# First expert layer of a graph network kernel: other PSUM banks, fewer unread products, result relus one group later

## The reference

```python
idx = argmax(norm(x) @ router_w.T + router_b)
h = relu(norm(x) @ W1[idx] + b1[idx])
x = x + relu(h @ W2[idx] + b2[idx])
```

## Time and profile before

| what | us |
|---|---|
| median of 3 runs (3088.12 to 3096.96) | 3088.62 |
| the profiled execution's own time | 3107.93 |
| its span | 3106.2 |
| from the first second product of the loop to the last, 19 steps from group to group (1905.00 to 2047.12) | 142.12 |

### The profile page before, as it was taken

One profiled execution on the slowest core, in us unless ns is written; L12 is line 12 of the kernel. 1 busy time (PEld: TensorE's weight loads), 2 busy tenths in 40 slices (PEclk: granted clock), 3 DMA queues, 4 the chain that ended last, 5 costly groups with the idle time before them and its releaser, 6 DMA issues. The chain is left out here.

```text
span 3106.2 us, 49414 instructions
## 1 busy us (share of the span) xinstructions
PE 2079.5 (67%) x13355; PEld 1574.6 (51%) x13356; DVE 1801.6 (58%) x4427; ACT 1371.4 (44%) x3064; POOL 1564.0 (50%) x1492
## 2 busy tenths in 40 slices
PE   8999116655565555655566546857133599999998
PEld 5555004443344433443444444645133388988887
DVE  5422226666565565665566884345488686656565
ACT  4555125554454544545454123523134664444443
POOL 0066645666666666666662313543650155555554
PEclk9999557777777877776777657978555599999999
DMA  7577434444444444444441632565442162222332
GB/s 232 206 269 280 158 90 110 131 122 116 126 123 120 130 119 123 127 119 120 122 121 37 168 107 82 140 140 133 98 114 65 35 183 49 45 47 46 49 48 27
DMA packets 194692, 363.31 MB, mean 117 GB/s; under 512 B 52783, under 2 KB 127126, under 8 KB 187983
## 3 DMA queue, kind: packets, MB, share of 16 engines
q0 software_dynamic: 78160, 187.31, 25.2%
q1 hardware_dynamic: 106126, 171.10, 16.5%
q10 hardware_dynamic: 10240, 2.95, 0.4%
HBM read 246.22 MB, written 117.28 MB: 117 GB/s over the span
## 5 line engine op out<-in xcount | busy, mean ns | idle before, releaser
L834 POOL DMA_INDIRECT sum_ring<-h_tab,gnn_edge_row x880 | 837.7, 952 | 484.9 <-issue 244.8
L1107 PE MATMUL sum_bank<-sum_ring,sum_one_hot 128*128 128x264 f32 x1760 | 619.0, 498 | 218.0 <-DVE nodes_acc L971 110.6
L1107 PEld LDWEIGHTS sum_bank<-sum_ring,sum_one_hot 128*128 128x128 f32 x1760 | 402.5, 244 | 348.9 <-issue 276.5
L878 ACT ACTIVATE sum_one_hot_T<-sum_distance,sum_pick_unit 128x1024 f16<-128x1024 bf16 x110 | 126.3, 1148 | 625.7 <-remote 616.8
L2243 POOL DMA_INDIRECT out_dram<-moe_y,slots_nodes x112 | 193.3, 1726 | 259.7 <-ACT moe_y L2265 237.7
L964 DVE TENSOR_TENSOR sum_ring<-sum_ring,sum_bank 128x1024 f32<-128x1024 f32 x220 | 266.5, 1212 | 94.1 <-ACT sum_ring L906 93.1
L885 ACT ACTIVATE sum_distance_by_lane<-all_iota,gnn_minus_local 128x128 bf16<-128x128 f32 x880 | 267.4, 386 | 0.1
L2417 PE MATMUL moe_bank<-moe_w_high,slots_early 128*128 x896 | 245.0, 273 | 6.8 <-DVE moe_w_low L1745 6.8
L2417 PE MATMUL moe_bank<-moe_w_high,moe_hidden_low 128*128 x896 | 245.1, 274 | 0.0
L2417 PE MATMUL moe_bank<-moe_w_low,slots_early 128*128 x896 | 245.1, 274 | 0.0
L2234 POOL DMA_INDIRECT moe_tile<-normal,slots_rows x116 | 136.4, 1176 | 188.5 <-PEq L71 134.5
(11 more groups left out here) (451 smaller groups left out, 4555.8 us busy)
## 6 DMA issues: line engine op xcount, KB each, us to landing
h_tab<-rows_h_rows SPq DMA_DIRECT2D x49, 1056.0 KB
sum_local_rows<-local_tab SPq DMA_DIRECT2D x110, 256.0 KB
slots_stage<-in_L_ffn_W_dram SPq DMA_DIRECT2D x14, 1024.0 KB
sum_ring<-h_tab,gnn_edge_row POOLq DMA_INDIRECT x880
mask_tab<-rows_masks POOLq DMA_DIRECT2D x7, 1560.0 KB
sum_masks<-mask_tab SPq DMA_DIRECT2D x28, 390.0 KB
results<-moe_tiles SPq DMA_DIRECT2D x80, 128.0 KB
g_tab<-gnn_rows_out SPq DMA_DIRECT2D x49, 132.0 KB
```

The costliest lines, as they stand in the source:

```text
L834: nc.gpsimd.indirect_dma_start(ring[:, t % (RING * ST), :], None, k.h_tab, bass.IndirectOffsetOnAxis(k.edge_row[:, t:t + 1], 0)).then_inc( ...
L1107: last = nc.tensor.matmul(sum_b[j][:, 0:W0], hot[:, m % 3, t, :], ring[:, m % RING * ST + t, :], start=(u == 0), stop=(u == G - 1))
```

## The change

The change touches `moe0` alone. The eight PSUM banks are given out anew: four to the transposes (bank u), two to the hidden values (bank 4 + u % 2), two to the second products (bank 6 + u % 2). So a tile's first products wait for the hidden relu of the tile two before (`h_ok.slot(n + u + 2)`), and its second product for the addition of the tile two before (`y_add.slot(n + u + 2)`); transposes no longer wait for additions, and second products no longer for the next group's splits. Of the unread products one is left ahead of the first products and two ahead of the second products, the latter now ahead of the wait for the hidden relu. `y` has eight slots, four of them in the space of the raw first weights. ACT's result relus are those of the group before, behind the columns of the next; the first two groups stand outside its loop, which then takes two groups in a turn, and the last four result relus stand behind the loop. DVE makes three splits, the first addition, the last split, and then the other three additions. SP's stores go round eight slots.

```diff
--- before.py
+++ after.py
@@ -1392,7 +1392,9 @@
         rows_ok = s.sem("slot_rows_ready")
         den = flat(route.work[:, :, :])[:, 0:NT * H0].rearrange("p (t h) -> p t h", h=H0)
         space = s.sb("tiles", [P, 12, D])
-        y, xi = (space[:, j * 4:(j + 1) * 4, :] for j in range(2))
+        xi = space[:, 4:8, :]
+        y_rows = [space[:, 0:4, :], flat(w1_in[:, :, :, :])[:, 0:4 * D].rearrange("p (u f) -> p u f", u=4)]
+        y = lambda u: y_rows[u // 4][:, u % 4, :]
         xT = [space[:, 8 + 2 * j:10 + 2 * j, :].rearrange("p u f -> p (u f)").bitcast(F16).rearrange("p (u f) -> p u f", u=4) for j in range(2)]
         spare = flat(route.pick[0][:, :, :])[:, 0:4 * D].rearrange("p (u f) -> p u f", u=4)
         taken = lambda u: (xi if u < 4 else spare)[:, u % 4, :]
@@ -1400,6 +1402,7 @@
         xn, xnT = space[:, 0:XN, :], space[:, XN:XN + 2, :]
         rw_n, rw = s.sb("router_natural", [E0, D]), s.sb("router", [P, DC, E0])
         rb = s.sb("router_bias", [P, E0])
+        x_bank, h_bank, y_bank = (lambda u: bank[u]), (lambda u: bank[4 + u % 2]), (lambda u: bank[6 + u % 2])
         w2 = s.sb("w2", [F0, E0, D])
         b1_n, b1, b2 = s.sb("b1_rows", [E0, F0]), s.sb("b1_T", [F0, E0]), s.sb("b2", [P, E0, D])
         x = b2[:, 0:AHEAD * CH, :].rearrange("p (n t) f -> p n t f", n=AHEAD)
@@ -1411,7 +1414,7 @@
         written = [s.sem(f"xn_written{u}") for u in range(XN)]
         route_ok, w1_hi, w1_ok = s.sem("route_ready"), s.sem("w1_high"), s.sem("w1_split")
         tile_in = [s.sem(f"tile_loaded{u}") for u in range(8)]
-        out_ok = Landed(s, "y_written", 4)
+        out_ok = Landed(s, "y_written", 8)
         x_ps = Count(s, "x_in_psum", 8)
         x_hi, x_ok, h_ps, h_ok, y_ps, y_add, y_ok = (Count(s, n, 4) for n in (
             "xT_high", "xT_split", "hidden_T_in_psum", "hidden_T_ready", "y_in_psum", "y_biased", "y_ready"))
@@ -1462,9 +1465,9 @@
             sp.dma_start(flat(b2[:, :, :]), v.broadcast_to([P, v.shape[1]])).then_inc(loaded_b, 16)
 
             def save(i, u):
-                y_ok.done(sp, i * 4 + u)
-                sp.dma_start(rows(k.ys0, (i * 4 + u) * P, P), y[:, u, :]).then_inc(out_ok.sems[u], 16)
-            turns(sp, T, 4, save)
+                y_ok.done(sp, i * 8 + u)
+                sp.dma_start(rows(k.ys0, (i * 8 + u) * P, P), y(u)).then_inc(out_ok.sems[u], 16)
+            turns(sp, T, 8, save)
             out_ok.all(sp, T)
 
         @block.scalar
@@ -1497,19 +1500,31 @@
 
             def columns(t, u):
                 x_ps.done(act, t)
-                nc.scalar.activation(xT[0][:, u, :], bank[2 * u + 1][:, D:2 * D], ACT.Copy, scale=XS).then_inc(x_hi.sem, 1)
+                nc.scalar.activation(xT[0][:, u, :], x_bank(u)[:, 0:D], ACT.Copy, scale=XS).then_inc(x_hi.sem, 1)
             for u in range(4):
                 columns(u, u)
-            with act.Fori(0, T // 4) as i:
-                e = registers(nc, mybir.EngineType.Activation, route.expert[0:1, bass.ds(i * 4, 4)], E0 - 1)
+            def rectify(t, u):
+                y_add.done(act, t)
+                nc.scalar.activation(y(u), y(u), ACT.Relu).then_inc(y_ok.sem, 1)
+
+            def group(n, half):
+
+                e = registers(nc, mybir.EngineType.Activation, route.expert[0:1, n:n + 4] if isinstance(n, int) else route.expert[0:1, bass.ds(n, 4)], E0 - 1)
                 for u in range(4):
-                    h_ps.done(act, i * 4 + u)
-                    nc.scalar.activation(hT[:, u, :], bank[2 * u][0:F0, 0:P], ACT.Relu, bias=col(b1, e[u]), scale=1.0 / (XS * WS)).then_inc(h_ok.sem, 1)
+                    h_ps.done(act, n + u)
+                    nc.scalar.activation(hT[:, u, :], h_bank(u)[0:F0, 0:P], ACT.Relu, bias=col(b1, e[u]), scale=1.0 / (XS * WS)).then_inc(h_ok.sem, 1)
                 for u in range(4):
-                    columns(i * 4 + 4 + u, u)
-                for u in range(4):
-                    y_add.done(act, i * 4 + u)
-                    nc.scalar.activation(y[:, u, :], y[:, u, :], ACT.Relu).then_inc(y_ok.sem, 1)
+                    columns(n + 4 + u, u)
+                if not isinstance(n, int) or n:
+                    for u in range(4):
+                        rectify(n - 4 + u, (4 * half + 4 + u) % 8)
+            for half in range(2):
+                group(half * 4, half)
+            with act.Fori(1, T // 8) as i:
+                for half in range(2):
+                    group(i * 8 + half * 4, half)
+            for u in range(4):
+                rectify(T - 4 + u, 4 + u)
 
         @block.vector
         def _(v):
@@ -1594,17 +1609,23 @@
 
             def column_rest(t, u):
                 x_hi.done(v, t)
-                nc.vector.scalar_tensor_tensor(xT[1][:, u, :], bank[2 * u + 1][:, D:2 * D], XS, xT[0][:, u, :], ALU.mult, ALU.subtract).then_inc(x_ok.sem, 1)
+                nc.vector.scalar_tensor_tensor(xT[1][:, u, :], x_bank(u)[:, 0:D], XS, xT[0][:, u, :], ALU.mult, ALU.subtract).then_inc(x_ok.sem, 1)
             for u in range(4):
                 column_rest(u, u)
-            with v.Fori(0, T // 4) as i:
-                e = registers(nc, mybir.EngineType.DVE, route.expert[0:1, bass.ds(i * 4, 4)], E0 - 1)
-                for u in range(4):
-                    column_rest(i * 4 + 4 + u, u)
-                for u in range(4):
-                    y_ps.done(v, i * 4 + u)
-                    out_ok.slot(v, i, u)
-                    nc.vector.tensor_tensor(y[:, u, :], bank[2 * u + 1][:, 0:D], col(b2, e[u]), ALU.add).then_inc(y_add.sem, 1)
+            def add(i, n, u, slot, expert):
+                y_ps.done(v, n + u)
+                out_ok.slot(v, i, slot)
+                nc.vector.tensor_tensor(y(slot), y_bank(u)[:, 0:D], col(b2, expert), ALU.add).then_inc(y_add.sem, 1)
+            with v.Fori(0, T // 8) as i:
+                for half in range(2):
+                    n = i * 8 + half * 4
+                    e = registers(nc, mybir.EngineType.DVE, route.expert[0:1, bass.ds(n, 4)], E0 - 1)
+                    for u in range(3):
+                        column_rest(n + 4 + u, u)
+                    add(i, n, 0, half * 4, e[0])
+                    column_rest(n + 7, 3)
+                    for u in range(1, 4):
+                        add(i, n, u, half * 4 + u, e[u])
 
         @block.tensor
         def _(pe):
@@ -1651,36 +1672,35 @@
                 u = slot % 4
                 pe.wait_ge(tile_in[slot], (i + 1) * 16)
                 for c in range(DC):
-                    last = nc.tensor.transpose(bank[2 * u + 1][:, D + c * P:D + (c + 1) * P], taken(slot)[:, c * P:(c + 1) * P], k.ident[:, :])
+                    last = nc.tensor.transpose(x_bank(u)[:, c * P:(c + 1) * P], taken(slot)[:, c * P:(c + 1) * P], k.ident[:, :])
                 last.then_inc(x_ps.sem, 1)
 
-            def unread(m):
+            def unread(to, m):
 
                 for _ in range(m):
-                    nc.tensor.matmul(bank[0][:, P:2 * P], k.ident[:, :], k.ident[:, :], start=True, stop=True)
+                    nc.tensor.matmul(to, k.ident[:, :], k.ident[:, :], start=True, stop=True)
 
             def four(n, i, half):
 
                 e = registers(nc, mybir.EngineType.PE, route.expert[0:1, bass.ds(n, 4)], E0 - 1)
                 for u in range(4):
-                    h_ok.slot(pe, n + u)
+                    h_ok.slot(pe, n + u + 2)
                     if u == 0:
-                        unread(2)
+                        unread(h_bank(u)[:, P:2 * P], 1)
                     x_ok.done(pe, n + u)
                     for part, (pw, px) in enumerate(passes):
                         for c in range(DC):
-                            last = nc.tensor.matmul(bank[2 * u][0:F0, 0:P], col(w1[pw][:, c], e[u]), xT[px][:, u, c * P:(c + 1) * P],
+                            last = nc.tensor.matmul(h_bank(u)[0:F0, 0:P], col(w1[pw][:, c], e[u]), xT[px][:, u, c * P:(c + 1) * P],
                                                     start=(part == 0 and c == 0), stop=(part == 2 and c == DC - 1))
                     last.then_inc(h_ps.sem, 1)
                 for u in range(4):
-                    y_add.slot(pe, n + u)
                     turn(i + half, 4 * (1 - half) + u)
                 for u in range(4):
+                    y_add.slot(pe, n + u + 2)
+                    if u == 0:
+                        unread(y_bank(u)[:, D:D + P], 2)
                     h_ok.done(pe, n + u)
-                    if u == 0:
-                        unread(4)
-                    x_ok.done(pe, n + 4 + u)
-                    nc.tensor.matmul(bank[2 * u + 1][:, 0:D], hT[:, u, :], col(w2, e[u]), start=True, stop=True).then_inc(y_ps.sem, 1)
+                    nc.tensor.matmul(y_bank(u)[:, 0:D], hT[:, u, :], col(w2, e[u]), start=True, stop=True).then_inc(y_ps.sem, 1)
             for u in range(4):
                 turn(0, u)
             with pe.Fori(0, T // 8) as i:
```

## The result

| | us |
|---|---|
| median after, 5 runs (3105.29 to 3119.86) | 3113.09 |
| median before, 5 runs (3086.71 to 3096.96) | 3088.62 |
| ratio | 1.008, 95% interval 1.0062 to 1.0098 |
| profiled execution after (span 3103.5) | 3105.29 |

The change costs 24.5 us. The profiled executions don't show that in their spans: the one of before took longer than any of its five timed runs (3107.93), the one of after is the shortest of its five. The rest of the program differs by more than the change between two executions, so the loop has to be compared with the loop. The 18 steps that took 132.26 before take 159.40 now, 27.1 more. The two groups ahead of them are 2.9 shorter in this execution and the tail behind them is 1.1 longer, so that the stage, from its first gather to the next stage's first load, takes 192.98 in place of 167.60, 25.4 more.

The account below looks back on a forecast made before the run. The tile loop, 7.35 us a group, was taken as set by a hold after each fourth gather. With release, relu, return and remaining products a group became 7.9; 0.55 more over 19 intervals gave +10.5, so 3099 us, range 3074 to 3118.

Parts of the forecast that it names:

- the hold: Work handed on by PE waits until about a microsecond after a group's fourth gather; now on first products, group 7.9 us.
- release at 6.54: The held hidden relu of tile 0 was to be let go 6.54 us after the group's transposes began.
- First transpose to second product 1.5: Start of a group: transposes and two unread products were to take 1.5 us in place of 2.60, so −1.1.
- Product 2 at 1.41: Second products: product 2, waiting for tile 0's addition, was to start 1.41 us into their phase.
- Without gathers about 7: The last stretch of the loop without gathers was to take about 7 us, not 6.25.
- the tail: End of the loop: the last four result relus were to follow the last additions as before, at no cost.
- the second products: With two banks, their phase was to take 2.6 us in place of 2.01, +0.6 a group.
- what follows the release: Relu and return 0.41 us, tile 3 0.36 after tile 2, next transposes 0.44 to 0.66 later.
- The lead that the sequencer loses: PE's sequencer at the expert numbers: 0 to +0.5 us a group, taken as +0.25, giving 7.05 without a hold.
- the clock: Rival: more PE pauses lower the granted clock below 1.00, 2.5 us more a group, +48, 3136 us; chance 0.09.
- Faster: Rival: the hold concerns additions alone and falls into slack, groups of 6.8, −10.5, 3078 us; chance 0.26.
- No difference: Rival: new relays cost what removed waits give, 7.3 a group, 3088 to 3093 us; chance 0.24.

Follow-up runs that it names:

- e2: Changed kernel with hidden values four deep again, turned tiles in pairs in two banks, second products still two deep: ratio 0.9993, steps of 7.36 us.
- e5: Changed kernel without its gathers of tiles, POOL only counting up: steps of 7.30 us, ratio 0.997, later layers working on other values.
- e3: Changed kernel with second products four deep again, turned tiles in pairs in two banks, hidden values still two deep: ratio 1.0068, steps of 8.48 us.
- e12: Changed kernel with four more unread products a group, put ahead of tile 2's first products where PE stops: ratio 1.007, steps of 8.61 us.
- e10: Changed kernel with hidden values and second products four deep, turned tiles and hidden values in pairs, six unread products: ratio 0.9941, steps of 6.66 us.
- e11: The four-deep arrangement with three unread products a group instead of six: ratio 0.9941, steps of 6.67 us.
- e9: Kernel before with only the result relus a group later and eight rows of y: ratio 0.9973, steps of 7.09 us.
- e14: Changed kernel with a group's gathers in two bursts of two: 3095.47 us against 3089.99 for before, one run each, steps of 7.83 us.
- e7: Changed kernel with hidden values four deep, second products two deep and six unread products: ratio 1.0005, steps of 7.63 us.

## Why the prediction was right, and too small

The sign, the place and the mechanism held; the size, 10.5, was less than half of the 24.5 measured, and one sign that the prediction gave for being wrong, a granted clock under 1.00, did show. The step as the prediction put it was: the hold falls on the first products, tile 2 can't start before the hidden relu of tile 0, release at 6.54, group 7.9. e2 (this relay undone) gives the whole loss back, e5 (the gathers taken away) gives it back in the steps of the loop, and e3 shows that PE merely waits longer there when it comes earlier.

*Terms that held.* First transpose to second product 1.5: 1946.59 − 1945.12 = 1.47. Product 2 at 1.41: 1947.99 − 1946.59 = 1.40. Release at 6.54: 6.59. Without gathers about 7: 7.05 (e5: 7.03 to 7.34 at a clock of 1.00).

*Put at nothing: the tail.* From the last group's second products to the next stage's first load it took 2054.08 − 2047.12 = 6.96 before and takes 2059.84 − 2051.78 = 8.06 now, 1.1 us more, once.

*Mis-sized without effect: the second products.* Their phase was put at 2.6 and takes 1949.69 − 1946.59 = 3.10. The first two tiles are still through PE before the release, so the group doesn't show it.

*Mis-sized: what follows the release.* Relu and return were put at 0.41; they take 1952.31 − 1951.71 = 0.60, since PE goes on 0.24 after the relu's end and not 0.05. From tile 2 to the next transposes I had 0.36 + 0.44 to 0.66, that is 0.80 to 1.02; at a clock of 1.00 it takes 1945.12 − 1944.00 = 1.12. The sum becomes 6.59 + 0.60 + 1.12 = 8.31, which e12 shows at 8.33 to 8.40. These 0.4 a group are some 8 us of the 19 steps. The lead that the sequencer loses was counted in the sum without a hold and left out of the sum with it.

*Mis-judged: the clock.* Its chance was 0.09 with 48 us; it fell in 13 of 18 steps, and cost little. The same 25 instructions take 2.59 at 1.00 and 3.71 at 0.58, but most of that is time that the release would have taken anyway: groups measured at their transposes take 8.54 to 8.65 where the clock falls and e12's 8.33 to 8.40 where it doesn't, about 0.25 for each. Two groups in the trace took 10.5 us from transposes to transposes, at a clock of 0.50 throughout. Together the clock would account for what is left, some 9 of 27 us; this last split is a subtraction and no run isolates it. The rule of the Trainium skill, page "TensorE: Matmul & The Clock Gate", section "A second HAM failure mode: psum-queue depth-cycling", agrees with this case: with two banks in turn PE paused, and the clock swung (13 low steps; none in e10 and e11, with both four deep). The 48 us that I hung on it were not borne out.

*What was luck.* The range left the falling clock out, and the measured 3113 lies 5 us under its top end. That end, 8.9 a group, was 6.8 and the additions' idle 2.07 on top; the 8.86 measured are mostly the corrected 8.31 and the clock. The two agree by chance.

*The rivals.* "Faster" rested on the hold touching the additions alone; the relu at 1951.71 refutes it. "No difference" is refuted for the whole, but it is what e2 measures, with the one relay undone. That the label "DMA" at the held additions named no store is shown by e9, where the additions are held with eight rows of `y` too, and by the changed kernel, where hidden relus, which wait for no store, are released at 6.59.

## What to carry to other kernels

A buffer's depth should be judged against the longest irregular hold, not the mean time of the engine that frees it: two banks cost PE a wait of 0.34 to 0.38 us where the relu of 0.36 us came at once, and one of over a microsecond where it came a microsecond late, in nearly every group. Look for what an engine stands behind at the time of the hold; e10 left the hold in place and won 0.59% by leaving one short wait for it. Where steps alternate between long and short, measure the period at another instruction before pricing either.

## What the runs showed of the hardware that was not expected

- What PE hands on is seen late by ACT and DVE around a run of four gathers. In the changed kernel the hidden relu comes 1.14 to 1.25 us after the end of the fourth, in every group in which it was ready by then; in the kernel before, the waiting addition comes 1.14 to 1.26 after it in 14 of 18 groups, 0.45 to 0.60 in four; in e14, with two and two, the hidden relus that still wait come 0.63 to 0.77 after the fourth. The hold can begin earlier: in nine of e10's 18 groups an addition is held that was due before the third gather began, and comes 0.97 to 1.11 after the end of that one.
- SP is held as well, and not by PE. The result relus of the group shown end at 1946.67 + 1.35 = 1948.02, and the four stores behind them take 4.56 us to issue, until 1951.84; in the last group, without gathers, the same four take 2.29. So the hold isn't only one of PE's signals. Why it is so stays open; e14 moves it and doesn't explain it.
- The granted clock fell with PE at 0.86 of the time in records and a stop of about a microsecond in each group, and in four steps of e7 with PE at 0.93 (127.86 of 137.35) and pauses of 0.28 to 0.39 in the steps read. It stayed at 1.00 in e10 with the same 0.93 (111.79 of 119.79) and a pause of 0.49 in the group shown, and in e11 with 0.85 (102.49 of 120.02). So neither the busy share of the profile nor a single pause told in these runs whether it falls.
